# A three-layer interaction network with an MLP: the first stream through all its layers ahead of the second, and another spread of the gathers

## The reference

```python
def _L0_rec_ref(embeddings, W0, W1, W2):
    x0 = embeddings
    xk = x0
    outs = []
    for W in (W0, W1, W2):
        xk = jax.nn.relu(jnp.einsum('bmd,bhd,mhk->bkd', x0, xk, W))
        outs.append(jnp.sum(xk, axis=2))
    return jnp.concatenate(outs, axis=1)

h = jnp.concatenate([z, dense_ctx], axis=1)
h = jnp.maximum(h @ W_top1 + b_top1, 0.0)
h = jnp.maximum(h @ W_top2 + b_top2, 0.0)
y = h @ W_top3
```

## Time and profile before

| | |
|---|---|
| Median of three runs | 698.55 us (698.49 to 698.56) |
| Profiled execution, its own time | 699.1 us |
| Its span, first to last instruction | 697.3 us |
| TensorE matmuls (PE) busy | 581.6 us, 83% |
| VectorE (DVE) busy | 569.7 us, 82% |
| GpSimd (POOL) busy | 453.7 us, 65% |
| ScalarE (ACT) busy | 231.7 us, 33% |
| Mean granted TensorE clock, as a share of full speed | 0.973 |

### The profile page before, as it was taken

How to read it: one execution, slowest core, us unless ns; L and a number is a source line. 1 busy time by engine, 2 the same in 40 slices (tenths; PEclk the granted TensorE clock), 3 DMA queues, 4 the chain that set the end, 5 groups by cost and what they waited for, 6 DMA issues and landing times.

```text
span 697.3 us, 7219 instructions
## 1 busy us (share of the span) xinstructions
PE 581.6 (83%) x2752; PEld 199.7 (29%) x2752; DVE 569.7 (82%) x295; ACT 231.7 (33%) x425; POOL 453.7 (65%) x348
## 2 busy tenths in 40 slices
PE   0040788999899989999899979998999989999978
PEld 0010222223332323323332324232332333233424
DVE  0020899998899998898889898898889889999963
ACT  0100361433325162615224242616243331616031
POOL 6776016188966978487948888487948896636120
PEclk9995799999999999999999999999999999999989
DMA  5498639059591949368672949195855949193000
GB/s 152 153 392 313 259 136 351 1 174 363 174 360 36 379 151 378 127 213 324 249 285 90 398 129 394 63 329 206 310 224 158 377 148 386 24 384 124 1 0 0
DMA packets 54244, 151.95 MB, mean 218 GB/s; under 512 B 9697, under 2 KB 18913, under 8 KB 54210
## 3 DMA queue, kind: packets, MB, share of 16 engines
q1 hardware_dynamic: 46018, 149.39, 57.1%
q0 software_dynamic: 8192, 2.11, 2.4%
HBM read 147.26 MB, written 4.20 MB: 217 GB/s over the span
## 4 chain that ended last, share of the span: by engine, by line
POOL 43%; issue 29%; PE 17%; DVE 3%; ACT 3%; POOLq 2%; SPq 1%; DMA 1%; DVEq 0%
POOL emb L281 25%; POOL zg L293 18%; PE acc L474 15%; DVE zd L360 3%; POOLq L292 2%; ACT xk_sb L389 1%; ACT xk_ps L389 1%; DMA z2d_y<-dense_t_in 1%; PE mlp L515 1%; ACT relu_ab L396 0%; PE mlp L506 0%; PE mlp L507 0%; PE acc L482 0%; DVE zpart L340 0%; PE mlp L562 0%
## 5 line engine op out<-in xcount | busy, mean ns | idle before, releaser
L360 DVE TENSOR_TENSOR zd<-rolled,xk_ps 128x2048 f32<-128x2048 f32 x244 | 543.9, 2282 | 112.5 <-issue 41.8
L474 PE MATMUL acc<-zd,w_sb 128*64 128x512 f32 x1696 | 401.0, 605 | 60.1 <-issue 33.5
L293 POOL TENSOR_TENSOR zg<-rolled,xk_sb 128x1024 f32<-128x1024 f32 x88 | 208.9, 2379 | 152.9 <-ACT xk_sb L389 151.8
L281 POOL DMA_INDIRECT emb<-tables_in,index x256 | 244.5, 955 | 69.2 <-issue 64.6
L474 PEld LDWEIGHTS acc<-zd,w_sb 128*64 128x64 f32 x1696 | 116.3, 138 | 317.7 <-issue 218.9
L389 ACT ACTIVATE xk_ps<-acc 64x512 f32<-64x512 f32 x128 | 73.0, 570 | 104.9 <-issue 52.9
L474 PE MATMUL acc<-zg,w_sb 128*64 128x512 f32 x352 | 91.4, 597 | 14.9 <-POOL zg L293 14.4
L474 PE MATMUL acc<-zd,w 128*64 128x512 f32 x256 | 63.0, 612 | 37.4 <-issue 36.7
L389 ACT ACTIVATE xk_sb<-acc 64x512 f32<-64x512 f32 x128 | 75.7, 591 | 3.1
L396 ACT ACTIVATE relu_ab<-acc 128x512 f32<-128x512 f32 x48 | 28.7, 597 | 122.7 <-issue 72.1
L474 PEld LDWEIGHTS acc<-zg,w_sb 128*64 128x64 f32 x352 | 23.8, 136 | 70.7 <-POOL zg L293 35.6
(11 more groups left out here) (46 smaller groups left out, 69.9 us busy)
## 6 DMA issues: line engine op xcount, KB each, us to landing
rolled<-x_scratch SPq DMA_DIRECT2D x256, 512.0 KB
base<-x_scratch SPq DMA_DIRECT2D x16, 512.0 KB
emb<-tables_in,index POOLq DMA_INDIRECT x256
x_scratch<-emb SPq DMA_DIRECT2D x32, 128.0 KB
w_sb<-w_in SPq DMA_DIRECT2D x2, 512.0 KB
wt<-wtop_in SPq DMA_DIRECT2D x1, 512.0 KB
wt1a<-wtop_in SPq DMA_DIRECT2D x1, 256.0 KB
w<-w0a_in SPq DMA_DIRECT2D x1, 160.0 KB
```

Source lines behind the costliest of these rows:

```text
L281: pool.indirect_dma_start(emb[:, i % 2, c * DIM:(c + 1) * DIM], None, tables, bass.IndirectOffsetOnAxis(index[:, g:g + 1].bitcast(U32), 0) ...
L293: nc.gpsimd.tensor_tensor(zg[:, n % ZG_BUFS, :], rolled[:, s, j, :], xk_sb[:, s, :], ALU.mult).then_inc(zg_ready, 1)
L360: nc.vector.tensor_tensor(zd[:, n % ZD_BUFS, 0:w, :], rolled[:, s, j:j + w, :], repeated(xk_ps[:, s, :], w), ALU.mult).then_inc(zd_ready, 1)
L474: end = nc.tensor.matmul(acc[h * MAPS:(h + 1) * MAPS, s, :], weights, z[:, h * HALF:(h + 1) * HALF], start=(i == 0 and c == 0), stop=(i == ...
```

## The change

- `ORDER` begins (0,0), (0,1), (0,2), (1,0), (1,1): stream 0 goes through its three layers first. The groups of six are as before.
- `POOL_CHUNKS`: per tile GpSimd has 4 chunks of (2t,1), 4 of (2t+1,1), 2 of (2t,2) and 2 of (2t+1,2), where it had 4, 2, 4 and 2. In the first two streams it has 10 chunks where it had 4.
- Gathers: 24 first, then a wait for VectorE's two products of stream 0's layer 0, then 4. All others stand behind products, by a table for (stream's parity, layer).
- `base_to_ps` of a stream stands two phases ahead of its layer 0. In the groups of six this is the place it had; only stream 1's moves, behind the evacuation of (0,1).
- `zsum` moves behind its phase, `mlp2` from two thirds of phase k = 5 to behind its first product, `mlp3` from behind that phase to two thirds of it. On ScalarE `zsum_to_sb` follows the evacuation of its phase, and `y_to_sb` goes ahead of the evacuation of k = 5.

```diff
{DIFF}
```

More of the change, by code:

```diff
@@ L42 @@
 DMA_RING = 8192
-ORDER = [(0, 0), (0, 1), (1, 0), (0, 2), (1, 1)]
+ORDER = [(0, 0), (0, 1), (0, 2), (1, 0), (1, 1)]
 for _t in range(1, TILES):
@@ L50 @@
 HEAD = 5
-POOL_CHUNKS = {(0, 0): 0, (1, 0): 0, (0, 1): 4, (1, 1): 2, (0, 2): 4, (1, 2): 2}
-POOL_CHUNKS_FIRST = {(0, 0): 0, (1, 0): 0, (0, 1): 0, (1, 1): 2, (0, 2): 0, (1, 2): 2}
+POOL_CHUNKS = {(0, 0): 0, (1, 0): 0, (0, 1): 4, (1, 1): 4, (0, 2): 2, (1, 2): 2}
+POOL_CHUNKS_FIRST = {(0, 0): 0, (1, 0): 0, (0, 1): 2, (1, 1): 4, (0, 2): 2, (1, 2): 2}
 SUMS_AFTER = [5, 5, 4]
-GATHERS_FIRST = 51
-GATHERS_BEFORE = 5
-GATHERS_AFTER = {1: [4, 5], 2: [1, 1, 1, 5], 4: [3, 1, 1, 1], 5: [2, 2]}
+GATHERS_FIRST = 24
+GATHERS_EARLY = 4
+GATHERS_AFTER = {(1, 2): [2, 3], (0, 1): [2, 2, 2, 4], (0, 2): [2, 2], (1, 1): [3, 3, 2, 5]}
+GATHERS_AFTER_FIRST = {(1, 2): [2, 3], (0, 1): [3, 5], (0, 2): [2, 2], (1, 1): [3, 3, 2, 5]}
 class Plan:
@@ L306, in _ @@
             gathers(GATHERS_FIRST)
[L307 to L310, removed]
+            pool.wait_ge(zd_ready, len(PLAN.dve[0]))
+            gathers(GATHERS_EARLY)
+            for q, (stream, layer) in enumerate(ORDER):
                 if PLAN.pool[q]:
@@ L315, in _ @@
                     product(q, n, j)
-                    if k in GATHERS_AFTER:
-                        gathers(GATHERS_AFTER[k][x])
+                    gathers((GATHERS_AFTER if stream > 1 else GATHERS_AFTER_FIRST)[stream % 2, layer][x])
         @block.vector
@@ L419, in _ @@
             base_to_ps(0)
[L420 to L423, removed]
+            for q in range(len(ORDER)):
                 k = (q - HEAD) % 6 if q >= HEAD else None
@@ L427, in _ @@
                     act.wait_ge(const_in, const_count)
[L428 to L434, removed]
+                if k == 4:
+                    h1_to_sb(m)
+                if k == 5:
+                    h2_to_sb(m)
+                    y_to_sb(m)
                 evacuate(q)
[L436 to L439, removed]
+                if k == 2:
+                    zsum_to_sb(m)
+                if q + 2 < len(ORDER) and ORDER[q + 2][1] == 0:
+                    base_to_ps(ORDER[q + 2][0])
             act.wait_ge(last_z01_done, 1)
@@ L458, in _, with phase @@
         def _(pe):
-            def phase(q, between=None):
+            def phase(q, **between):
                 stream, layer = ORDER[q]
@@ L483, in phase @@
                                              xk_sb[:, s, h * HALF:(h + 1) * HALF], start=False, stop=False)
-                    if between is not None and i == len(merged) * 2 // 3:
-                        between()
+                    if "early" in between and i == 0:
+                        between["early"]()
+                    if "late" in between and i == len(merged) * 2 // 3:
+                        between["late"]()
             def half_sums(m, dst, layer):
@@ L539, in _ @@
                 phase(q + 1)
-                phase(q + 2, lambda: zsum(m))
+                phase(q + 2)
+                zsum(m)
                 phase(q + 3)
[L542 to L545, removed]
+                phase(q + 4, late=lambda: mlp1(m))
+                phase(q + 5, early=lambda: mlp2(m), late=lambda: mlp3(m))
+            phase(len(ORDER) - 1, late=last_sums)
             m = TILES - 1
```

## The result

The changed kernel takes 801.75 us (798.0 to 804.6), the kernel before 698.52 us in the same session: a ratio of 1.148, 95% interval [1.142, 1.153]. The profiled execution took 804.6 us, its span is 802.5. It is slower, as forecast, but by 103 us and not 68; the forecast of 767 us and its range, up to 790, missed the time.

A forecast was written before the change was run, and what follows sets the result against it. Late gathers, through ScalarE's base copies, bound the loop: halves of 39.6 and 46.6 us plus 2.0 for the clock make 88.2 a tile; six tiles after 168.6 plus 68.3 give span 766.0, forecast 767 us, own range 752 to 786, 718 to 790 with the first rival.

The forecast's parts named there:

- The start: Program start: no long gather train at 44.04, so ScalarE's first evacuation moves from 68.50 to 44.1.
- R1: Moment in each tile when xk_sb of the odd stream's layer 1 is ready; first forecast at 128.0, against 136.3 before.
- the hole: Start: ScalarE's evacuation waits from 44.04 to 68.50 during 51 gathers; forecast gone; rival that it stays: 24.4 us more, 0.12.
- The feed: Each stream's last gathers now stand behind more GpSimd products, ending 25.15 us after R1 and 26.37 after R2.
- Half 1: Tile part from R1 to R2: late gathers, base load and copy, then the evacuation, 39.6 us.
- The first rival (PE not held): Feed late, but h2 gets past ACT in time, so mlp3 does not hold PE: 733 or 721 us; chance 0.12.
- faster: Rival: loads early enough all the same, first R1 at 116.0, six PE waits of 1.6 us go: 669 us; chance 0.08.
- the edits costed at nothing: GpSimd's product split, zsum and mlp2 moves, six DVE chunks moved to GpSimd: no separate cost; PE wait bounds 0 to -1.6 us a tile.
- R2: Moment in each tile when the even stream's layer 1 xk_sb is ready; first forecast at 168.6, last at 697.7.
- The clock in half 2: PE's clock may fall after its wait of about 5 us for h2: up to 2.9 us more, bound only.
- the clock's fall in half 1: PE's clock falls after about 7 us idle, making xk_sb of (2t+1,0) 2.0 us late; counted in the tile.
- half 2: Tile part from R2 to the next R1: gathers, base copy, h2, mlp3, rest of (2t+1,1), evacuation, 46.6 us.

The follow-up runs named there:

- kernel with nine gathers ahead: Changed kernel with 11 gathers instead of 2 behind GpSimd's last product of (0,2): 677.3 us beside 673.1 for the kernel before, ratio 1.005.
- old kernel with a late feed: Kernel before with 42 gathers ahead of the first phase instead of 51, all else as it was: 756.4 us beside 673.7, ratio 1.124.

## Why the prediction was wrong in size

- **The start was right.** Evacuation forecast at 44.1, measured 44.19; GpSimd's (1,1) at 96.7, measured 97.34; R1 of the first tile at 128.0, measured 128.24. Its reason was half right: the hole goes with the train, but in half the sessions there is none to go.
- **The feed was right.** Half 1 was to take 39.6 us, and 226.45 to 265.86 are 39.4. The 7.43 us from the last gather to the base copy held (203.39 to 210.88 is 7.49), and base copy, h2 and mlp3 stand in the order forecast. The first rival (PE not held) is out by the wait of 7.54 us, and "faster" is what the kernel with nine gathers ahead would have been with the old start.
- **The step that failed: "SP does not hold the feed back: its waits are on products made long before", and with it the new split of GpSimd's chunks, which stands among the edits costed at nothing.** SP's waits held nothing here: it issued the sixteen loads of stream 3 from 161.9 to 172.3. What the forecast left out is their order. SP loads a stream's chunks in the order in which the slot's layer 2 uses them, and the new split changes this order. By the kernels' plans, from stream 3 on, the chunk with which GpSimd begins a layer 1 was the fifth load of an even stream and the seventh of an odd one; now it is chunk 12 in both, the fifteenth of sixteen. As long as the feed is early this costs nothing. With a late base GpSimd waits for it. Two rows of the timelines before that wait, and GpSimd's waits of this kind in all (us, times, longest):

```profile
180.24 0.94 POOL L283 DMA_INDIRECT emb<-tables_in,index  x1 [0.30 <-issue]
...
180.47 2.44 ACT L390 ACTIVATE xk_sb<-acc 64x512 f32<-64x512 f32 x4
...
POOL zg L295 <- DMA rolled<-x_scratch: 47.0, 8, 10.1
```

  After 180.24 + 0.94 = 181.18 GpSimd waited until 186.55, 5.4 us. The forecast had 2.0 us there, for xk_sb, which was ready at 182.91, after 1.7; so 3.4 were missing, then on the path to the next gathers. At 142.98 the same wait made the first R2 3.1 us late, 171.67 instead of 168.6. The old kernel with a late feed, which has the old split, has no such wait, and the changed kernel with GpSimd's four chunks loaded right behind the first four, 774.7 us, has none either and is 27 us faster.
- **The clock in half 2 was a bound and not in the sum.** From mlp3 (213.54) to the evacuation (221.56) are 8.0 us at a granted clock of 0.62, where the forecast had 5.1 at full clock. The upper bound that I gave, 2.9 us, is what came. The 2.0 us of the clock's fall in half 1 came out near, at 1.7, though the case from which they were read is less clear than the forecast said: in stream 0's layer 0 the profile's granted clock is 1.00 from 36 to 44, while the first eight matmuls take 3.68 us and the last eight 2.15.
- **The sum.** 48.6 + 3.4 + 2.9 = 54.9, and half 2 from 171.67 to 226.45 is 54.78. Later tiles are a little shorter: 93.3 against the forecast 88.2, six times 5.1 = 30.7. With 3.1 at the first R2, and 70.9 instead of 68.3 behind the last, it is 36.4 us: 802.4 for the span, measured 802.5. The forecast's own range ended at 786: it held a clock fall in each half (784) but not the load, and 3.4 us more in each of six tiles would have been 20 us past that.

## What to carry to other kernels

Where a producer is spread behind the consumer's own work, count its lead in program positions first: nine gathers out of 32 a tile decided between 677 and 801 us, and a late start is paid again in each round. When a feed turns late, go through everything that it brings and in which order, and through what is queued behind its waits on every engine; a split of work between two engines can set that order without a word about loads. Nearly half of the loss, 57 of 128 us, sat in two waits (h2 behind the base copy, the chunks needed first loaded last) that cost nothing while it was early. A kernel's time before is a measurement in one session: the same program had 25 us more or less at its start.

## What the runs showed of the hardware

- In some sessions a train of gathers on GpSimd goes with late releases of one engine by another, in others the same program doesn't see it: first evacuation at 68.50, 69.61 or at 43.85, beside 51 gathers. SyncE is not held meanwhile: it issues the load of stream 1's base at 53.86 with the hole and at 53.93 without. It goes with the hole that h2 started 2.2 us late in six tiles, during a train of seven gathers. In the session without the hole it starts with PE's end in these tiles too, and the tile is 76.9 us either way:

```profile
332.82 0.62 ACT L412 ACTIVATE h<-mlp,bt 128x128 f32<-128x128 f32 x2 [9.55 <-PE mlp L515]
```

- No row speaks for the fetch of code as its cause. Between 44 and 68.5 the DMA view of the kernel before has two queues, neither of them one of instructions, as q8 and q14 are on its page:

```profile
q1 hardware_dynamic: 2423, 8.04, 86.6%
q0 software_dynamic: 625, 0.16, 3.8%
```

  By the rule of the Trainium skill (Runtime: NRT & Kernel Launch, Instruction fetch mechanics) that each sequencer fetches its instructions through a DMA queue of its own, code that is fetched there would show as such packets; the trace agrees with the forecast's reading that it is none, as far as these two queues show the fetch of every engine.
- Memsets of 0.13 us between the gathers did not end the hold; behind a wait of GpSimd ahead of a short train there was none: with GpSimd idle for 6.9 us until 39.68 and four gathers behind that, ScalarE was released at 42.75, in the midst of the four.
